# A batched graph attention layer on one Trainium2 core: the mean of all nodes as a bias of an output copy, the feature bias by an adding DMA, and the sum of h over row blocks on TensorE

## The reference

```python
h = einsum('bnd,ade->bane', x, W)                  # 12 heads, 32 features each
th = tanh(h)
attn = leaky_relu(th @ w_src + (th @ w_dst).T, 0.2)  # per head, 512 x 512
attn = where(~adj, -999.0, attn)
attn = softmax(attn, axis=-1)
feat_out = elu(einsum('banm,bame->bane', attn, h) + b)
gate = sigmoid(x @ H_w.T + H_b)
out = layernorm(x + gate * feat_out + (1 - gate) * x)
```

## Time and profile before

| quantity | value |
|---|---|
| median of three runs | 711.69 us (711.6 to 712.4) |
| profiled execution, its own time | 711.58 us |
| its span, first to last instruction | 709.8 us |
| busy share: PE, DVE, POOL, ACT | 96%, 96%, 85%, 58% |
| mean granted TensorE clock | 0.99 of full speed |
| one step in the middle of the run | 42.0 us |

### The profile page before, as it was taken

How to read it: one execution, slowest core, us unless ns; L and a number is a source line. 1 busy time by engine, 2 the same in 40 slices (tenths; PEclk the granted TensorE clock), 3 DMA queues, 4 the chain that set the end, 5 groups by cost and what they waited for, 6 DMA issues and landing times.

```text
span 709.8 us, 12409 instructions
## 1 busy us (share of the span) xinstructions
PE 678.0 (96%) x3327; PEld 376.1 (53%) x3327; DVE 678.3 (96%) x1225; ACT 412.4 (58%) x859; POOL 601.0 (85%) x434
## 2 busy tenths in 40 slices
PE   8899999999999999999999999999999999999882
PEld 5464655546555555555655554564646455554530
DVE  7699999999999999999999999999999999999996
ACT  5324558284664838567383765828476482855673
POOL 2964798998989899898989989899898989988393
PEclk9999999999999999999999999999999999999997
DMA  5253335263352615335261443426244351533402
GB/s 193 101 176 117 101 104 196 66 210 112 130 168 94 203 59 188 112 132 173 94 221 59 148 149 134 163 89 213 84 134 163 111 186 61 169 108 128 161 30 89
DMA packets 47083, 94.55 MB, mean 133 GB/s; under 512 B 2962, under 2 KB 28308, under 8 KB 47060
## 3 DMA queue, kind: packets, MB, share of 16 engines
q1 hardware_dynamic: 38868, 82.08, 35.5%
q10 hardware_dynamic: 8192, 12.19, 4.6%
HBM read 81.28 MB, written 12.98 MB: 133 GB/s over the span
## 4 chain that ended last, share of the span: by engine, by line
PE 72%; ACT 10%; DVE 7%; issue 5%; POOL 4%; DMA 2%; ACTq 0%; DVEq 0%; SPq 0%; POOLq 0%
PE out_T L976 37%; PE hg L898 28%; PE tr L984 4%; DVE ew L743 4%; ACT xT_hi L450 3%; ACT scratch L521 2%; ACT att_T L497 1%; PE hg L959 1%; ACT h_sb L462 1%; DMA xT_in<-in_xT 1%; DMA v_all<-v_rows 1%; DVE ex L778 1%; DVE att L761 1%; PE hg L931 1%; DVE att L772 1%
## 5 line engine op out<-in xcount | busy, mean ns | idle before, releaser
L743 DVE SCALAR_TENSOR_TENSOR ew<-v_all,u,adj 128x512 f32<-128x512 f32 x768 | 526.0, 732 | 0.5 <-DMA v_all<-v_rows 0.5
L976 PE MATMUL out_T<-ew,vals 128*64 128x512 f32 x1536 | 367.6, 602 | 2.7 <-DVE ew L743 2.7
L976 PEld LDWEIGHTS out_T<-ew,vals 128*64 128x64 f32 x1536 | 107.3, 137 | 198.3 <-issue 154.7
L301 POOL TENSOR_TENSOR th_w<-th,score_w 128x768 f32<-128x768 f32 x58 | 107.6, 1855 | 48.0 <-ACT th L458 40.8
L497 ACT ACTIVATE att_T<-out_T,tiny 128x512 f32<-128x512 f32 x96 | 65.8, 685 | 134.7 <-PE out_T L976 134.7
L898 PE MATMUL hg<-w_hi,xT_hi 128*128 128x384 f32 x384 | 99.4, 367 | 8.9 <-ACT h_sb L462 6.5
L898 PEld LDWEIGHTS hg<-w_hi,xT_hi 128*128 128x128 f32 x384 | 61.8, 191 | 50.6 <-issue 47.3
L898 PE MATMUL hg<-w_lo,xT_hi 128*128 128x384 f32 x384 | 88.6, 338 | 0.0
L898 PE MATMUL hg<-w_hi,xT_lo 128*128 128x384 f32 x384 | 87.6, 335 | 0.0
L305 POOL TENSOR_TENSOR th_w<-th_w 128x384 f32<-128x384 f32 x58 | 78.1, 1347 | 4.5
L468 ACT ACTIVATE gate_tanh<-hg 128x384 f32<-128x384 f32 x64 | 31.2, 490 | 78.3 <-PE hg L898 78.3
(11 more groups left out here) (106 smaller groups left out, 734.5 us busy)
## 6 DMA issues: line engine op xcount, KB each, us to landing
v_all<-v_rows SPq DMA_DIRECT2D x96, 512.0 KB, 3.8
xT_in<-in_xT SPq DMA_DIRECT2D x16, 768.0 KB, 4.6
x_in<-in_x SPq DMA_DIRECT2D x15, 768.0 KB, 4.5
out<-y ACTq DMA_DIRECT2D x15, 768.0 KB, 5.3
adj_in<-in_adjT SPq DMA_DIRECT2D x16, 256.0 KB, 4.9
xT_in<-in_x SPq DMA_DIRECT2D x1, 768.0 KB, 6.0
ew<-in_W SPq DMA_DIRECT2D x1, 576.0 KB, 4.2
gate<-in_HwT SPq DMA_DIRECT2D x1, 576.0 KB, 8.0
```

The lines of the kernel that those rows point to most:

```text
L301: g.tensor_tensor(th_w[:, c % 2], th[:, c].unsqueeze(1).broadcast_to([P, 2, D]), score_w[:], ALU.mult).then_inc(S["thw_done"], 1)
L743: ve.scalar_tensor_tensor(out=ew[:, (2 * C * j + i) % SLOTS, :], in0=v_all[:, j % VSLOTS, k], scalar=u[:, q, c, h:h + 1], in1=ADJ[c][:], o ...
L976: te.matmul(OUT[VW * k:VW * k + VW, :], vals[:, q, c, h, :], ew[:, t % SLOTS, :], start=(c == 0), stop=(c == C - 1)).then_inc(S["ew_free"], 1)
```

## The change

1. The copy of h (line 462) adds 1 on the way; POOL's `add_bias` becomes a DMA that POOL issues and that adds a row of biases from DRAM onto all of `h_sb` in place. It is issued after the last `weigh` of the step, and no longer after `mix`. `add_rows` is gone, and with it `hb_sum` and `hb_tot`.
2. `means` is no longer one matmul with 384 columns but 12 matmuls with one column each: the weights are blocks of 128 x 128 of `h_sb`, the moving operand is a column of `TINY / N`. Their result stands with the features on the partitions, three columns. It is computed for batch b + 1, at the same place on TensorE, and waits for the DMA.
3. ACT brings these columns into a bias tile, `out_bias`, with four small copies for each batch (`out_biases`), ahead of the first `copy_out`; the copies of outputs then add bias column j in place of `tiny`. `alone`, `add_means`, `means_alone` and their late forms are gone.
4. The exponential in `vals` is multiplied by `LIFT`, in an extra instruction of ACT, and `TINY` is larger.
5. At the end, ACT's exponential for the middle columns and DVE's steps for them move ahead of the last pair's.

The core of the diff (hunks of semaphore names, tile declarations and waits that only follow from these are left out):

```diff
-TINY = 1.2e-38
+TINY = 2.0 ** -90
+LIFT = 2.0 ** 60
...
-        mean_ps = HG[1][:, 0:D]
+        mean_ps = HG[1][:, D:D + H // 4]
...
-                sp.dma_start(bias_row[:], bias.rearrange("(o n) -> o n", o=1).broadcast_to([P, E])).then_inc(S["ld_rows"], 16)
...
-                g.memset(mean_w[:], 1.0 / N).then_inc(S["pool_setup"], 1)
+                g.memset(mean_w[:], TINY / N).then_inc(S["pool_setup"], 1)
...
-                pool.wait_ge(S["ld_rows"], 16)
-
-                g.tensor_scalar(bias_row[:], bias_row[:], 1.0, 1.0, ALU.mult, ALU.add).then_inc(S["pool_setup"], 1)
                 pool.wait_ge(S["pool_setup"], SETUP)
+                pool.wait_ge(S["hcopy_done"], C)
+                add_bias(0)
 
                 pool.wait_ge(S["scores"], 1)
-                add_bias(0)
                 for c in range(2):
                     split_low(1, 1, c)
                 pool.wait_ge(S["dve_setup"], DVE_SETUP)
                 values(0, 0)
-                add_rows(0, 0)
...
             def add_bias(b):
-                pool.wait_ge(S["hcopy_done"], C * b + C)
-                g.tensor_tensor(h_sb[:].rearrange("p c (h e) -> p (c h) e", e=E), h_sb[:].rearrange("p c (h e) -> p (c h) e", e=E),
-                                bias_row[:].unsqueeze(1).broadcast_to([P, C * H, E]), ALU.add).then_inc(S["hb_done"], 1)
-
-            def add_rows(b, q):
-                pool.wait_ge(S["hb_done"], b + 1)
-                g.tensor_tensor(hb_sum[:], h_sb[:, 0:2], h_sb[:, 2:4], ALU.add).then_inc(S["hb_sum_done"], 1)
-                pool.wait_ge(S["hb_sum_done"], 2 * b + 1)
...
-                g.tensor_tensor(hb_tot[:, q], hb_sum[:, 0], hb_sum[:, 1], ALU.add).then_inc(S["hb_sum_done"], 1)
+                pool.dma_start(h_sb[:].rearrange("p c d -> p (c d)"), bias_rows, accum_op=ALU.add).then_inc(S["add_bias_done"], 16)
 
             def values(b, q):
-                pool.wait_ge(S["hb_done"], b + 1)
-                pool.wait_ge(S["exps_done"], NEX * b + 1)
+                pool.wait_ge(S["add_bias_done"], 16 * b + 16)
+                pool.wait_ge(S["exps_done"], NEX * b + 2)
...
                     for c in range(2 if first else 0, C):
                         weigh(b + 1, c)
+                if not last:
+                    add_bias(b + 1)
                 if not first:
                     subtract_x(b - 1)
                     mix(b - 1)
                 if not last:
-                    add_bias(b + 1)
-                    add_rows(b + 1, 1 - q)
                     values(b + 1, 1 - q)
...
-                a.activation(h_sb[:, c], feature_bank(b, c)[:, 0:D], ACT.Copy).then_inc(S["hcopy_done"], 1)
+                a.activation(h_sb[:, c], feature_bank(b, c)[:, 0:D], ACT.Identity, bias=plus1[:, 0:1]).then_inc(S["hcopy_done"], 1)
...
-                a.activation(vals[:, q, :, :, E], d_rel[:], ACT.Exp, scale=ALPHA).then_inc(S["exps_done"], 1)
+                a.activation(s_pos[:], d_rel[:], ACT.Exp, scale=ALPHA).then_inc(S["exps_done"], 1)
+                act.wait_ge(S["exps_done"], NEX * b + 1)
+                a.activation(vals[:, q, :, :, E], s_pos[:], ACT.Copy, scale=LIFT).then_inc(S["exps_done"], 1)
...
+            def out_biases(b):
+                act.wait_ge(S["hm_done"], b + 1)
+                if not isinstance(b, int) or b:
+                    act.wait_ge(S["outT_copied"], HP * b)
+                m = out_bias[:].rearrange("p (i s) -> p i s", s=2)
+                for r in range(4):
+                    rows = slice(VW * (r % 2), VW * (r % 2) + E)
+                    a.activation(m[rows, :, r // 2], mean_ps[E * r:E * r + E, :], ACT.Copy).then_inc(S["out_bias_done"], 1)
...
-                a.activation(att_T[:, j % 2], OUT[:], ACT.Identity, bias=tiny[:, 0:1]).then_inc(S["outT_copied"], 1)
+                if j == 0:
+                    act.wait_ge(S["out_bias_done"], 4 * b + 4)
+                a.activation(att_T[:, j % 2], OUT[:], ACT.Identity, bias=out_bias[:, j:j + 1]).then_inc(S["outT_copied"], 1)
...
+                if not first:
+                    out_biases(b)
                 copy_out(b, 0)
...
-                means_alone()
                 row_sums(b - 1)
                 copy_out(b, 3)
                 exp_early(q)
                 copy_out(b, 4)
                 row_squares(b - 1)
+                exp_late(q, 0, MIDDLE)
                 copy_out(b, 5)
...
-                        ve.tensor_scalar(alone[:], t[:, :, 0, E], TINY, None, ALU.is_le).then_inc(S["alone_done"], 1)
                     ve.reciprocal(rden[:], t[:, :, :, E]).then_inc(S["inv_done"], 1)
...
-            def add_means(b, q):
-
-                dve.wait_ge(S["att_done"], HP * b + HP)
-                dve.wait_ge(S["hm_done"], b + 1)
-                dve.wait_ge(S["alone_done"], b + 1)
-                for c in range(C):
-                    ve.scalar_tensor_tensor(out=att[:, q, c], in0=mean_ps, scalar=alone[:, c:c + 1],
-                                            in1=att[:, q, c], op0=ALU.mult, op1=ALU.add).then_inc(S["att1_done"], 1)
...
-                dve.wait_ge(S["mean_last_done"], C)
-                add_means_late(MIDDLE, HP * B - 1)
+                dve.wait_ge(S["gate1_done"], B)
+                elu_late(0, MIDDLE)
                 dve.wait_ge(S["y_early_done"], 2)
                 statistics(0, EARLY)
                 inverses()
                 quotients()
-                add_means_late(FINAL, HP * B)
-                elu_late(0, MIDDLE)
+                gated(MIDDLE, 1)
                 elu_late(1, FINAL)
+                gated(FINAL, 2)
                 y = y_last[:, :, LATE]
-                dve.wait_ge(S["elu_late_done"], 2)
-                ve.tensor_tensor(y, y, gate[:, :, LATE], ALU.mult).then_inc(S["y_late_done"], 1)
-                dve.wait_ge(S["y_late_done"], 1)
+                dve.wait_ge(S["y_late_done"], 2)
                 ve.tensor_tensor(y, y, rest_last[:, :, LATE], ALU.add).then_inc(S["y_late_done"], 1)
...
                 transpose_v(0)
+                means(0)
                 warm_up(WARM)
...
-            def means(b, q):
-                pe.wait_ge(S["hb_sum_done"], 2 * b + 2)
-                pe.wait_ge(S["gate_done"], C * b + C)
-                te.matmul(mean_ps, mean_w[:, 0:1].broadcast_to([P, P]), hb_tot[:, q], start=True, stop=True).then_inc(S["hm_done"], 1)
+            def means(b):
+                pe.wait_ge(S["add_bias_done"], 16 * b + 16)
+                if not isinstance(b, int) or b:
+                    pe.wait_ge(S["gate_done"], C * b)
+                for i in range(H // 4):
+                    for c in range(C):
+                        last = te.matmul(mean_ps[:, i:i + 1], h_sb[:, c, i * P:(i + 1) * P], mean_w[:, 0:1],
+                                         start=(c == 0), stop=(c == C - 1))
+                last.then_inc(S["hm_done"], 1)
...
                 attend(b, q, 4)
 
-                means(b, q)
+                if not last:
+                    means(b + 1)
                 transpose_out(b, 4)
                 attend(b, q, 5)
...
-        "bias": np.asarray(L0_gnn_b),
+        "bias": np.tile(np.asarray(L0_gnn_b), (x.shape[1] // 128 * H, 1)),
```

More of the change, by code:

```diff
@@ L38, in gat_layernorm @@
     SLOTS = 16
-    SETUP = 13
+    SETUP = 12
     DVE_SETUP = 12
@@ L104, in gat_layernorm @@
         rden = sb("rden", [P, C, 2])
-        alone = sb("alone", [P, C])
         att = sb("att", [P, 2, C, D])
@@ L150, in gat_layernorm @@
         NSC = 4
-        NEX = 4
+        NEX = 5
         EARLY = slice(0, 3 * VW)
@@ L607, in x_last_form @@
                 a.activation(x_plus1[:], x_last, ACT.Identity, bias=plus1[:, 0:1]).then_inc(S["x_forms_done"], 1)
-            def means_alone():
-                act.wait_ge(S["hm_done"], B)
-                act.wait_ge(S["alone_done"], B)
-                for c in range(C):
-                    a.activation(mean_last[:, c], mean_ps, ACT.Copy, scale=alone[:, c:c + 1]).then_inc(S["mean_last_done"], 1)
             def exp_early(q):
                 y = y_last[:, :, EARLY]
-                act.wait_ge(S["att_last_done"], 1)
+                act.wait_ge(S["att_done"], HP * (B - 1) + 3)
                 act.wait_ge(S["mixed"], 3 * (B - 1) + 3)
@@ L805, in step @@
                     edges(b, q, j, between)
-                    if j == 0 and not first:
-                        add_means(b - 1, 1 - q)
             def after():
@@ L914, in features @@
                         pe.wait_ge(S["vT_done"], b)
-                    elif c > 1:
+                    elif c == 1:
+                        pe.wait_ge(S["out_bias_done"], 4 * b)
+                    else:
                         pe.wait_ge(S["hcopy_done"], C + c - 1)
@@ L919, in features @@
                 elif c == 3:
-                    pe.wait_ge(S["att1_done"], C * (b - 1))
+                    pe.wait_ge(S["out_bias_done"], 4 * b)
                 else:
```

55 lines of the change are left out of this document (23 added, 32 removed).

## The result

The changed kernel takes 765.99 us (762.14 to 766.14, four runs) where the kernel before takes 712.05: a ratio of 1.074 [1.071, 1.078], slower by 54 us. The forecast was 733 us, with a range up to 758. The direction was right and the size was not.

A forecast was written before the change was run, and what follows sets the result against it. The prediction took TensorE's own path to bound the kernel. To 711.58 us it added +25.5 (TensorE), -3 (DVE), +0.5 (start) and -1.5 (end), +21.5 in all: 733 us, forecast 715 to 745, range 706 to 758.

The forecast's parts named there:

- DVE's gain: Without `add_means`, the reciprocal of j = 0 starts right behind the transposition: 0.2 us a step, -3 us; bounds nothing to -12.
- ACT's part: Four small copies ahead of the first output copy and one more exponential step: nothing; without cover 0.4 us a step.
- the start: `means(0)` waits for the DMA and adds 2.7 us, mostly falling into the first attend's wait: +0.5 us, between -1 and +5.
- the clock: Rival, chance 0.17: each block of one-column matmuls brings a clock dip, 1.7 us more a step, 758 us.
- the sum's own upper bounds: Upper bounds of the terms added to the profiled time: 711.6 + 53 + 5 = 770 us.
- What bounds the kernel: The chain of waits runs almost only on TensorE, at its own pace for 40.6 of a step's 41.98 us.
- TensorE's part: The mean's 24 load and matmul pairs at 0.111 us delay the transpositions: +1.7 us a step, +25.5 us (+8 to +53).
- POOL's part: Addition and two sums gone, 6.45 us a step, off the chain: nothing; the DMA needs 9 us and has 17.8.
- The end: DVE loses a 1.95 us addition and a short one, an ELU takes the first's place: -1.5 us, between -3 and 0.

The follow-up runs named there:

- run 12: The changed kernel with the mean taken over two of four row blocks, 12 pairs a step in place of 24: 729.23 us, 1.023.

## Why the prediction was right or wrong

The time came out 33 us above the forecast and 8 above the range. Four steps of the prediction failed: DVE's gain, which didn't come; ACT's part, put at nothing; the start, mis-sized; and the clock, kept out of the sum as a rival on the ground that weight loads may count as work. The range's upper end, 758, was the clock's figure alone. It left no room for these coming together, though the sum's own upper bounds reached 770.

**What bounds the kernel: right.** TensorE's path did, and the work spared on DVE and POOL bought nothing.

**TensorE's part: right.** +1.7 us a step was forecast, +1.74 measured; the 0.111 us a pair taken from the weight loads was 0.112. The 81 ns of the Trainium skill ("TensorE: Matmul & The Clock Gate", Back-to-back issue gap), which would have given +1.0, was too low for these float32 pairs.

**DVE's part: wrong.** "The gain that arrives is only that the reciprocal starts right behind the transposition", 0.2 us a step: the reciprocal did start there, and the run without `add_means` gained nothing (711.79 against 711.94). The step that failed was to add up DVE's work from the transposition to the last tile at its lengths in the trace. The ELU's 2.29 us were not its own length: it takes 1.75 with POOL idle, and the rest was waiting for POOL's product, so an earlier start only made it longer.

**ACT's part: wrong.** "Nothing; without that cover 0.4 us a step" counted slack only against the transposition of j = 0. Who else waits for ACT was not asked: the second wait goes from `th` over POOL's product to the ELU. It cost 0.28 us in attend j = 1, and moving the copies away gave 0.48 a step. The copy of h with its bias, 0.57 us against 0.49, wasn't priced, and is most of the 0.14 ahead of the second feature block; no run takes it alone. Together these are 0.4 us a step, 6 us in all.

**POOL's part: right.** The DMA landed in 6.5 us where 9 were taken, and 17.8 were there for it.

**The clock: the rival came true in part,** as an addition to the forecast. It had been priced at 1.7 us in each of 15 steps; six steps lost 13.6 us together, one to three each. The step that failed is the clock of 1.00 throughout the middle, on which the sum stands; the reason given for it, that weight loads may count as work, had no row.

**The start: mis-sized,** +9.7 against +0.5 and a bound of +5. The prediction let the delay fall into attend 0's own wait, but that wait is for tiles that DVE makes behind `w_lo`, and it moved along with everything else. It did not follow ACT's queue, in which `w_hi` stands behind the wait for the means (6.54 us), nor take the block at the lower clock, 5.15 us in place of 2.7. With the clock at 1.00 the same order cost 3 us, inside the bound; the other 6.6 came with the late DMA and the clock.

**The end.** +1.5 us was measured behind the means of the last inner step, which holds one more block (+1.7) and one more attend j = 1 (+0.3). So the end gained about half a microsecond (2.0 - 1.5), inside its bounds and less than the 1.5 taken.

In all: the 25.5 forecast for the load stood; 3 of gain did not come, and 6 of ACT's cost, 9 at the start, 13.6 of clock and 1 at the end were missing.

## What to carry to other kernels

Before an instruction's length is used in a sum, compare it with the same instruction elsewhere in the trace: a part of it may be a wait for a port, and such a wait keeps its end when the start moves. A slow engine that shares a port with a critical one sets its order, and so does whoever releases the slow one; the cheapest repair is to put the long instruction where the critical engine idles anyway. A one-column float32 matmul was not nearly free here: each of its two pairs cost 0.11 us, and many of them in one block took the clock down as well. Let an idle engine do such a sum, or spread the pairs.

## What was unexpected of the hardware

A block of 24 pairs, back to back for 2.8 us with TensorE never idle, brought the granted clock down behind it in 6 of 14 steps (0.70 over 8 us, attend 5 from 3.73 to 5.97 us); in the middle of the run 12 pairs in one block, or the same 24 in three pieces, did not. DVE's ELU, with both operands in SBUF, takes 1.75 us alone, 2.3 to 3.4 when it starts behind an instruction of POOL's, and when it is first by 0.01 us it makes POOL's 1.01 us into 2.62. An adding DMA of 768 KB landed in 6.5 us (median), against 4.6 for the plain load of `x_in`; the plain load of `xT_in`, of the same size, took 6.3 in the same run, so no run here tells what the adding costs.
